# Unrolled normalising stages, weights made between batches, and a down product by token rows

## The reference

```
x = x + conv_0(norm_over_nodes(x, eps=1e-6))
t = tokens(x);  t = t + experts(norm_over_nodes(t, eps=1e-5)) # 2 of 8 experts per token
x = x + conv_1(norm_over_nodes(x, eps=1e-6))
t = tokens(x);  t = t + bitlinear(relu(bitlinear(norm(t), w_up))**2, w_down)

norm:      (v - mean) / sqrt(var + eps)         # over the 512 nodes
conv:      channel attention, time attention, a node-by-node attention times A,
           times W_gcn, a convolution over time with 3 taps (tcn_w) and bias,
           plus a 1x1 convolution (res_w), relu, layer norm over channels
bitlinear: quantise each token's row to 8 bits by its own maximum, multiply with
           weights rounded to -1, 0, 1; multiply by the row's and the weights' scale
```

## Time and profile before

| | us |
|---|---|
| median of three runs | 1845.0 (1844.95 to 1847.39) |
| profiled execution, its own time | 1845.8 |
| its span in the profile | 1844.0 |
| n0, from the first slab load to the last node copy | 8 to 92 |
| convolution weights, layer 0 and 1 | 92 to 99, 1182 to 1189 |
| m0 (16 batches) | 115 to 163 |
| g0 | 175 to 489 |
| n1 and router | 489 to 660 |
| experts | 660 to 1086 |
| join | 1086 to 1182 |
| g1 | 1270 to 1581 |
| ff | 1584 to 1844 |

### The profile page before, as it was taken

How to read it: one execution, slowest core, us unless ns; L and a number is a source line. 1 busy time by engine, 2 the same in 40 slices (tenths; PEclk the granted TensorE clock), 3 DMA queues, 4 the chain that set the end, 5 groups by cost and what they waited for, 6 DMA issues and landing times. The chain is left out here.

```text
span 1844.0 us, 28228 instructions
## 1 busy us (share of the span) xinstructions
PE 1435.7 (78%) x8462; PEld 1179.5 (64%) x8462; DVE 1119.4 (61%) x2438; ACT 751.4 (41%) x1181; POOL 636.5 (35%) x918
## 2 busy tenths in 40 slices
PE   4578899999364279999999944586999998277776
PEld 4457688888343268888888834384788887155554
DVE  4622488888465744444554325464688887488885
ACT  2412355555142033333333223221555554277674
POOL 1100065565410355555555431000255665211111
PEclk7678899999698579999999965587999999598887
DMA  6423012212375035565555376551022121122221
GB/s 202 145 79 93 9 61 76 69 60 69 102 223 172 1 114 114 103 132 119 117 114 119 42 184 208 182 173 35 18 77 68 60 77 61 60 72 82 77 77 60
DMA packets 96702, 179.97 MB, mean 98 GB/s; under 512 B 14160, under 2 KB 32128, under 8 KB 96644
## 3 DMA queue, kind: packets, MB, share of 16 engines
q1 hardware_dynamic: 72564, 135.52, 23.5%
q0 software_dynamic: 16384, 31.51, 10.0%
q10 hardware_dynamic: 7696, 12.22, 2.2%
HBM read 113.12 MB, written 66.10 MB: 97 GB/s over the span
## 5 line engine op out<-in xcount | busy, mean ns | idle before, releaser
L763 PE MATMUL g_y<-L_z,L_pt 128*128 128x192 f32 x1024 | 195.9, 335 | 1.5 <-ACT L_pt L976 0.5
L921 POOL TENSOR_TENSOR L_xr<-L_xr,L_lnb 128x192 f32<-128x192 f32 x128 | 105.9, 855 | 201.2 <-DMA L_xr<-x 105.9
L763 PEld LDWEIGHTS g_y<-L_z,L_pt 128*128 128x128 f32 x1024 | 165.7, 192 | 6.8 <-ACT L_pt L976 6.8
L1301 POOL DMA_INDIRECT sums<-x_yo,x_places x64 | 103.0, 1609 | 135.3 <-ACT x_yo L1504 125.3
L968 ACT ACTIVATE L_e<-g_s,L_nm 128x512 f32<-128x512 f32 x128 | 88.0, 688 | 79.1 <-DVE L_nm L809 78.0
L731 PE MATMUL g_z<-L_kw,L_xnT 96*128 96x192 f32 x512 | 97.0, 344 | 25.6 <-DVE L_v L839 25.5
L731 PEld LDWEIGHTS g_z<-L_kw,L_xnT 96*128 96x128 f32 x512 | 87.1, 198 | 37.7 <-DVE L_v L839 37.7
L928 POOL TENSOR_TENSOR L_t<-L_rstd 128x48 f32<-128x48 f32 x96 | 28.9, 301 | 235.3 <-DVE L_rstd L863 230.2
L1413 DVE TENSOR_TENSOR x_mid<-ex_g,x_sig 128x480 f32<-128x480 f32 (+1 forms) x48 | 31.3, 653 | 121.0 <-ACT x_sig L1495 114.5
L809 DVE TENSOR_REDUCE L_nm<-g_s 128x1 f32<-128x512 f32 x128 | 87.5, 684 | 26.6 <-PE g_s L740 25.8
L818 DVE SCALAR_TENSOR_TENSOR L_p<-L_e,L_rl,L_adj 128x512 f32<-128x512 f32 x128 | 99.5, 777 | 5.4 <-DVE L_rl L816 0.4
(11 more groups left out here) (313 smaller groups left out, 3855.8 us busy)
## 6 DMA issues: line engine op xcount, KB each, us to landing
xn_rows<-L_xnT SPq DMA_DIRECT2D x48, 384.0 KB, 3.5
L_xnT<-xn_rows SPq DMA_DIRECT2D x48, 384.0 KB, 3.4
x<-L_y SPq DMA_DIRECT2D x32, 384.0 KB, 2.6
L_xa<-in_x SPq DMA_DIRECT2D x16, 384.0 KB, 4.0
L_raw<-xn_rows SPq DMA_DIRECT2D x16, 384.0 KB, 3.4
L_xr<-in_x SPq DMA_DIRECT2D x16, 384.0 KB, 3.4
L_xa<-x SPq DMA_DIRECT2D x16, 384.0 KB, 3.9
sums<-L_raw ACTq DMA_DIRECT2D x16, 384.0 KB, 3.1
```

The source lines that it names most:

```text
L763: last = nc.tensor.matmul(out, pt[k % 2][:, P * c:P * c + P], z[q][:, c, :], start=False, stop=(c == NK - 1))
L921: last = nc.gpsimd.tensor_tensor(v_, v_, gain(s.lnb), ALU.add)
L1301: nc.gpsimd.indirect_dma_start(sums, row(places[e % 2][:, 1, t:t + 1]), yo[t % 4][:, :], None, compute_op=ALU.add).then_inc(sent[t % 4], 16)
```

## The change

- **Constants.** The stage `load_consts` goes. Inside n0, SP issues the identity, slabs 0 and 1, then the ten other constants, then slabs 2 and 3. TensorE waits for the identity alone, VectorE for the rest at batch 9.
- **normalise** is written out for all batches, without a loop. Slabs have four buffers, xn four, raw three; psx has three slots in n0 and two in n1. VectorE's statistics end in two aggregating instructions and one addition. In n0 the node copy is ScalarE's. xn is stored in two halves. The convolution's loads, now eleven, stand on SP's queue at batch 4.
- **Logits** are computed with the copied nodes stationary and wr moving (8 columns), two halves, all batches into one PSUM bank, copied once at the end, already by tokens. The transposes in `route` go, and its wait for constants stands some operations later.
- **ConvWeights**: the steps of `conv_weights` are placed between the batches of n0 and of the join, from batch 9 (8 in the join's VectorE) on; GpSimd clears the padded tensors of `graph_conv` behind its last root.
- **mix_channels** loads wt and A (`late_loads`) behind its first four slabs.
- **combine** is written out; x2 has three buffers and is stored from ScalarE's queue; slab b+4 is asked for ahead of the store of batch b.
- **feed_forward**: go_down(b, h) multiplies per half, token rows stationary and the down weights moving (512 columns); ScalarE scales its 96x512 result by the factor of each row (`scale_out`), TensorE turns it to nodes (`turn_out`, four transposes), VectorE adds the residual (`residual`).

```diff
+    def take(self, dve, ps):
+        dve.wait_ge(self.mix_done, 1)
+        self.nc.vector.tensor_copy(self.mixed, ps[0:HALF, 0:2, self.AT:self.AT + 4 * O]).then_inc(self.mix_taken, 1)
+        dve.wait_ge(self.mix_taken, 1)
+
+    def taken(self, pe):
+        pe.wait_ge(self.mix_taken, 1)
...
+                def load(b):
+                    since(sp, slab_turned, b - 3)
+                    sp.dma_start(xa[b % 4][:, :, :], src[b]).then_inc(xa_in[b % 4], 16)
+
+                if consts:
+                    consts.first(sp)
+                load(0)
+                load(1)
+                if consts:
+                    consts.rest(sp)
+                load(2)
+                load(3)
+                for b in range(B):
+                    if prefetch and b == 4:
+                        prefetch(sp)
+                    sp.wait_ge(xn_done, b + 1)
+                    for h in range(2):
+                        sp.dma_start(xn_rows[b][:, h, :], xn[b % 4][h]).then_inc(sent[b % 4], 16)
+                    if b + 4 < B:
+                        load(b + 4)
+                for z in range(4):
+                    sp.wait_ge(sent[z], B // 4 * 32)
+                if consts:
...
+                for b in range(D):
+                    turn_slab(b)
+                for b in range(B):
+                    if tail and b == tail.BATCH:
+                        since(pe, nodes_sb, b)
+                        tail.tensor(pe, psa)
+                        tail.taken(pe)
+                    if route:
+                        if b + D < B:
+                            turn_slab(b + D)
+                        turn_back(b)
+                        since(pe, nodes_sb, b)
+                        if b > 0:
+                            logits(b - 1)
+                    else:
+                        turn_back(b)
+                        if b + D < B:
+                            turn_slab(b + D)
+                if route:
+                    logits(B - 1)
...
+                for b in range(B):
+                    pool.wait_ge(var_done, b + 1)
+                    since(pool, xn_done, b - 1)
+                    root(nc, s, b % 2).then_inc(rstd_done, 1)
+                if tail:
+                    tail.gpsimd()
...
+                for b in range(B + 1):
+                    if route and b < B:
+                        keep_raw(b)
+                    if b < B:
+                        apply_norm(b)
+                    if route and b < B:
+                        send_raw(b)
+                    if not route and b > 0:
+                        copy_nodes(b - 1)
...
+                for z in range(4):
+                    sp.dma_start(xnT[z][0:HALF, :, :], xn_rows[z]).then_inc(xn_in[z], 16)
+                late_loads(sp, s, d, L, late)
+                with sp.Fori(1, B // 4) as i:
                     for z in range(4):
                         sp.wait_ge(mixed, free(i * 4 + z, 4))
                         sp.dma_start(xnT[z][0:HALF, :, :], xn_rows[i * 4 + z]).then_inc(xn_in[z], 16)
+                sp.wait_ge(late, 32)
...
-                for padded in (*u, *v):
-                    nc.vector.memset(padded[:, :].bitcast(F32), 0.0)
...
+                    load(b)
+                for b in range(B):
+                    if b == 3:
+                        prefetch(sp)
+                    if b + 4 < B:
+                        load(b + 4)
+                    sp.wait_ge(xn_done, b + 1)
+                    for h in range(2):
+                        sp.dma_start(xn_rows[b][:, h, :], xn[b % 3][h]).then_inc(sent[b % 3], 16)
+                for z in range(3):
+                    sp.wait_ge(sent[z], len(range(z, B, 3)) * 32)
...
+                turn_raw(0)
+                turn_raw(1)
+                for b in range(B):
+                    if b == tail.BATCH:
+                        since(pe, nodes_sb, b - 1)
+                        tail.tensor(pe, psa[b % 2])
+                        tail.taken(pe)
+                    turn_back(b)
+                    if b + 2 < B:
+                        turn_raw(b + 2)
...
+                for b in range(B):
+                    apply_norm(b)
+                    copy_x(b)
...
-                def spread_factors(b):
-
-                    pe.wait_ge(product_done, free(b, 1))
-                    pe.wait_ge(diag_done, ready(b))
-                    for h in range(2):
-                        last = nc.tensor.matmul(psd[:, h, 2 * CT:2 * CT + HALF], s.ones[0:HALF, :], diag[:, h, :],
-                                                start=True, stop=True)
-                    last.then_inc(factors, 1)
-
-                def go_down(b):
-                    pe.wait_ge(factors_sb, ready(b))
-                    pe.wait_ge(q2_sb, ready(b * 2 + 1))
+                def go_down(b, h):
+                    n = b * 2 + h
+                    pe.wait_ge(q2_sb, ready(n))
+                    pe.wait_ge(scaled, free(n, 1))
+                    for c in range(UK):
+                        last = nc.tensor.matmul(psd[0:HALF, :], q2s[:, c, HALF * h:HALF * h + HALF], wdn[:, c, :],
+                                                start=(c == 0), stop=(c == UK - 1))
+                    last.then_inc(down_done, 1)
+
+                def turn_out(b, h):
+                    n = b * 2 + h
+                    pe.wait_ge(scaled, ready(n))
+                    pe.wait_ge(out_done, free(n, 1))
                     for k in range(NK):
-                        for c in range(UK):
-                            last = nc.tensor.matmul(psd[:, k // 2, CT * (k % 2):CT * (k % 2) + CT],
-                                                    wdn[:, c, P * k:P * k + P], q2s[:, c, :],
-                                                    start=(c == 0), stop=(c == UK - 1))
-                    last.then_inc(down_done, 1)
-
-                def turn(b, q, i, first=True, second=True, third=True):
+                        last = nc.tensor.transpose(psf[:, HALF * k:HALF * k + HALF], od[h][:, P * k:P * k + P],
+                                                   s.ident[0:HALF, 0:HALF])
+                    last.then_inc(back_turned, 1)
+
+                def turn(b, q, i, first=True, second=True, third=True, fourth=True):
                     if first:
                         turn_slab(b + 2, q, i + 1)
                     if second:
                         go_up(b + 1, 1 - q, 0)
+                    if fourth:
+                        turn_out(b - 1, 1)
                     if third:
                         turn_q2(b, q, 0)
                         turn_q2(b, q, 1)
-                        spread_factors(b)
                     if second:
                         go_up(b + 1, 1 - q, 1)
                     if third:
-                        go_down(b)
+                        go_down(b, 0)
+                        go_down(b, 1)
                     if first:
                         turn_q1(b + 2, q)
-
-                turns(pe, turn)
+                    if third:
+                        turn_out(b, 0)
...
+                def down_factors(b, q):
+                    dve.wait_ge(scaled, free(2 * b + 1, 4))
+                    V.tensor_scalar(f2[q][:, :], am2[:, :], s.wscale[0:HALF, 1:2], None, ALU.mult).then_inc(factors, 1)
...
-                def product(b, q, i):
-                    dve.wait_ge(factors_sb, ready(b))
-                    dve.wait_ge(down_done, ready(b))
...
-                    for a in range(2):
-                        last = V.tensor_tensor(ya[q][:, 2 * a:2 * a + 2, :],
-                                               psd[:, a, 0:2 * CT].rearrange("p (k x) -> p k x", k=2),
-                                               fb[:, :].unsqueeze(1).to_broadcast([P, 2, CT]), ALU.mult)
-                    last.then_inc(product_done, 1)
...
+                def residual(b, q, h, i):
+                    dve.wait_ge(back_turned, ready(b * 2 + h))
+                    if h == 0:
+                        dve.wait_ge(xr_in[q], dma_ready(i))
+                        dve.wait_ge(sent[q], dma_free(i))
+                    in_time = lambda t: t.rearrange("p k (t c) -> p k t c", c=C)
+                    V.tensor_tensor(yo[q][:, :, :].rearrange("p k (c t) -> p k t c", t=T)[:, :, TH * h:TH * h + TH, :],
+                                    in_time(psf[:, 0:NK * HALF].rearrange("p (k x) -> p k x", k=NK)),
+                                    in_time(xr[q][:, :, HALF * h:HALF * h + HALF]), ALU.add).then_inc(out_done, 1)
...
-                    if third:
-                        product(b, q, i)
                     if first:
                         copy_q1(b + 2, q)
-
-                turns(dve, turn)
+                    if third:
+                        residual(b, q, 0, i)
...
+                def scale_out(b, q, h):
+                    n = b * 2 + h
                     act.wait_ge(factors, ready(b))
-                    nc.scalar.activation(fb[:, :].rearrange("p (h x) -> p h x", h=2),
```

(7 more changed lines are left out.)

670 lines of the change are left out of this document (320 added, 350 removed).

## The result

The changed kernel takes 1771.8 us, the median of four runs (1766.7 to 1773.9), against 1845.0 for the kernel before: a ratio of 0.9598, with a 95% interval of 0.9573 to 0.9622. In a later group of runs it came to 1769.8 and 0.9593 (0.9578 to 0.9608). The profiled execution took 1773.7 us, with a span of 1771.9, so 72.1 us less span than before. The forecast was 1786 us, with a range of 1764 to 1814.

The account below looks back on a forecast made before the run. Dependence chains or too few buffers were taken to bound the normalising stages and join, VectorE to be fullest in the feed-forward. Terms -29 - 25 - 4 - 3 - 4 + 2 + 4 = -59 gave 1786 us, range 1764 to 1814.

Parts of the forecast that it names:

- rival (b): Feed-forward: if VectorE sets the mean turn, it gains 0.9 us a turn, 1769 us in all; chance 0.15.
- the +2 of the sum: First normalising stage: eleven small loads on SP's queue ahead of batch 4's store add 2 us.
- the sign of being wrong that the prediction named: Normalising stages: the prefetch on SP's queue stops the stores for more than a batch.
- The bounds for a matmul of eight columns: n1 logits: between 0.05 and 0.18 us each, sixteen making 0.8 to 2.9 us a batch.
- the period of 4.85: n1: period of 4.85 us a batch in place of 5.11, giving -4 us, bounds -9 and +5.
- +0.7 at full clock, 13.2 becomes 13.9: Feed-forward: the longer path to copy_q1 adds a net 0.7 us to a full-clock turn of 13.2 us.
- 14.43 + 0.3: Feed-forward: mean turn goes from 14.43 to 14.7 us, +0.3 x 15 = +4 us.
- what would make it wrong: Whole kernel: signs against the forecast in n0's period, the join's waits, SP's prefetch, or a feed-forward clock moving from 0.84.
- (a): Normalising stages give half, n0 at 3.9, join 4.9 to 5.0, n1 5.1 us, about 1810 us; chance 0.2.
- (c): Feed-forward gets long at half rate, turn of 16.3 us, +28, whole still faster at 1810 us; chance 0.08.
- (d): Feed-forward: serial go_down near half clock makes the kernel slower than before, 1859 us at a 19.5 us turn; chance 0.03.
- (e): Unrolled loops still meet in one buffer; only start, reloads, weights and memsets go, about 1810 us; chance 0.09.

Follow-up runs that it names:

- The exchange on VectorE: Changed kernel with the shift of batch b-1 ahead of the node copy of batch b-2 on VectorE in the join: 1762.7 us, ratio 0.9552.
- the narrower product: Changed kernel with one of eight sum steps made for the last 128 of 512 down product columns in the feed-forward: 1782.1 us, a single run.

## Why the prediction was right, and where it was not

The kernel is faster by 73 us, 59 were forecast, and the time lies in the range. But the sum has two wrong signs in it, -10 for +4 and +8 for -4, which nearly cancel; that is luck. And 1771.8 lies nearer to the 1769 of rival (b) than to the forecast.

**Start, and first stage.** Forecast -29, measured -36.4 (99.22 to 62.78). The start was right: 4.54 us for 4.6. The steady period was mis-sized: 3.33 us was taken from TensorE's two groups in the earlier trace rows, 1.42 + 1.91, and those are durations of a mixed clock. With a denser row the clock was 1.00 in stretches, and the groups took 0.85 and 1.08. The limit was then VectorE's row with the wait on GpSimd, which the forecast had put at about 3.0 and which closed at 2.64. The weights went whole, as forecast (-7). The row of small loads came with a step of 7.7 in place of 2.6, so +5 for the +2 of the sum, and the sign of being wrong that the prediction named, stores stopped for more than a batch, did come (SP issued a store at 18.65 us and the next at 25.20). The weight matmuls at batch 9 cost +2.7 (5.3 for 2.6), for +3. The long step was put down to SP's queue alone, and the run with spread loads shows that the transfers' own time makes such a stop as well. Two PSUM slots cost 9.2 us, so the third slot was one third of the gain.

The rule of the Trainium skill that transposes don't bring the full rate (TensorE: Matmul & The Clock Gate, Part 4: PE-mode transpose) doesn't agree with this stage: between 5 and 26 us it had nothing but such turns, at a clock of 0.89 and 1.00, as these two windows of the changed kernel show:

```profile
5.00:20.00 15.00, 11.68 (x78) 10.01 (x77) 9.16 (x31) 8.03 (x12) 3.44 (x5) 0.89 0.76 232
20.00:26.00 6.00, 4.05 (x36) 3.18 (x34) 4.26 (x14) 4.99 (x8) 1.38 (x2) 1.00 0.85 254
```

It agrees with the join, at 0.50 before and after the change.

**Join.** Forecast -25, measured -27.2. The period was taken from the two undisturbed applies, 4.21, and was 4.20. This is the term of the sum with the best ground: the row showed the chain alone. The exchange on VectorE showed that the chain was the limit.

**n1.** Forecast -4, measured +7.8. The bounds for a matmul of eight columns, 0.05 and 0.18 us, held at both clocks (2.62/16 = 0.16 us at half, 1.52/16 = 0.10 at full). The step that failed is the period of 4.85: it took ScalarE's row and the two slots as the limit and TensorE's groups at the full clock of the earlier trace rows, and that clock was not given any more. With 1.91 + 1.49 + 2.62 us TensorE had almost no gap left and set the period, 5.8. The run with the old form shows it: same order, clock 0.90, 4.34. The period that the forecast named, 4.85, had thus been reached but for this form. The rule on stationary loads (the Trainium skill, TensorE: Matmul & The Clock Gate, LDWEIGHTS) gave an estimate of 1.3 us a batch. The shortest group of sixteen took 1.52, near it, those at half clock 2.62, twice as long: the trace agrees at full clock alone.

**Router.** Forecast -3, measured -5.5 in the opening and +1.1 behind it. The wait for the constants moved behind seven operations, and 1.1 us of it is left there.

**Memsets and late loads.** -1.9 and -2.0, as forecast. The late loads of the mix cost +0.1 in layer 0, where +1 was taken, and at most +1.0 in layer 1.

**Feed-forward.** Forecast +4, measured -9.9. The path was right: "+0.7 at full clock, 13.2 becomes 13.9" came out as 13.5, with TensorE waiting between the halves and turn_q1 behind the second. The failed step is the mean turn: 14.43 + 0.3 took the clock of before as given. It was not. In the kernel before it stood at 0.88 over ten turns, now at 1.00 over ten, and nearly all turns are at their full-clock length. Rival (b) named the right size of the turn (0.9 less, 1769 us in all) with the wrong cause. VectorE was in fact relieved by 0.9 us a turn (the residual's two additions take 0.83 us each where 0.51 was taken, but the rounding takes 0.68 where 1.02 was), and the narrower product lost the gain with the same relief. The point "what would make it wrong" did name it: a feed-forward clock that moves from 0.84.

So rivals (a) and (c) fell, (d) and (e) too. The forecast for the feed-forward was of the right mechanism at fixed clock; its sign was decided by the clock.

## What to carry to other kernels

- Take a period from the place in the trace where the chain runs undisturbed, as the last two batches of a stage: it predicted the join to 1%. Then look which queue's order closes the chain; moving one small operation ahead of a copy gave 6 us in the join and 12 in n1. Once it is open, look for the next loop and not only for the next full engine: in all three stages that was VectorE's row from shift to shift, with its wait for another engine in it.
- A duration on TensorE holds only for its granted clock, and an edit can change that clock in both directions. State a stage's time at both levels, and ask of each edit whether TensorE has more or less to multiply afterwards: here the form that moves more columns made the feed-forward faster, and the one that moves fewer made n1 slower. These are two cases, not a rule.
- A single accumulator shared by two halves costs what stands between its last write and its read. Where banks are short, the order on the reading engine is the next thing to try: one step earlier was worth 17 us here.

## What the runs showed of the hardware

- The granted clock of TensorE fell from 0.99 to 0.90 when a fifth of the down product was left out, and the stage grew from 244.1 to 250.0 us. In n1 it was 0.90 with the router weights stationary (eight records of 192 columns a batch) and 0.59 with the nodes stationary (sixteen records of 8 columns), though TensorE was busy 82.5 of 96 us there.
- A record of 8 moving columns with 96 stationary ones took 0.16 us at half clock and about 0.1 at full clock (1.52 us for sixteen in one batch), for a result that the other form made in eight records of 192 columns, 1.47 us.
- The transfers of this kernel reached 337 GB/s at a DMA share of 0.95, so 355 at a full share, where the forecast had worked with 314 and 318.
